# Split row maxima reach Q's rows through a scratch in memory instead of a TensorE transpose

## What is computed

```python
q, k, v = split(x @ W_attn + b_attn)                  # (8, 16, 1024, 32)
scores = einsum('bhki,bhqi->bhkq', k, q) / sqrt(32)   # keys before queries
scores = where(key <= query, scores, -10000.0)
attn = softmax(scores, axis=2)                        # over the keys
x = layernorm(x + combine(attn, v) @ W_out + b_out)
# then a block that routes the top half of the tokens of each of 4 pairs of
# sequences through a 512-2048-512 network, adds, and normalises again
```

## Time and profile before

| | |
|---|---|
| median of 3 runs | 2532.54 us (2531.82 to 2533.45) |
| span of the profiled execution | 2531.8 us |
| PE busy | 2456.4 us, 97% |
| PEld busy | 1817.1 us, 72% |
| DVE busy | 1658.1 us, 65% |
| POOL busy | 1568.4 us, 62% |
| ACT busy | 1191.0 us, 47% |
| DMA packets, data | 167502, 287.45 MB |

### The profile page before, as it was taken

The page is one execution under the profiler, slowest core; times in us unless marked ns, Lnnn a source line. Parts: engine busy times, 40 slices in busy tenths (PEclk is TensorE's granted clock), DMA queues, the critical chain, the costliest instruction groups (busy, mean ns, idle before and its releaser), DMA issues. The chain is left out here.

```text
span 2531.8 us, 40908 instructions
## 1 busy us (share of the span) xinstructions
PE 2456.4 (97%) x14168; PEld 1817.1 (72%) x14168; DVE 1658.1 (65%) x4230; ACT 1191.0 (47%) x2035; POOL 1568.4 (62%) x1642
## 2 busy tenths in 40 slices
PE   8999999999999999999999999997999999999997
PEld 6656676767777677777767667774788888888886
DVE  7767677677767777767787776775655544553533
ACT  3665566556566656656656565566521111111110
POOL 2878778788888788878788887875233122221311
PEclk9999999999999999999999999998999999999999
DMA  4233445335344433535434343443421001010000
GB/s 175 89 127 120 146 141 195 123 127 182 125 147 158 153 134 136 172 131 177 146 124 159 123 172 128 158 146 102 162 80 35 24 26 43 25 34 26 26 25 17
DMA packets 167502, 287.45 MB, mean 114 GB/s; under 512 B 23241, under 2 KB 58121, under 8 KB 166026
## 3 DMA queue, kind: packets, MB, share of 16 engines
q1 hardware_dynamic: 160130, 267.99, 30.2%
q0 software_dynamic: 7168, 16.85, 2.1%
HBM read 116.97 MB, written 65.11 MB: 72 GB/s over the span
## 5 line engine op out<-in xcount | busy, mean ns | idle before, releaser
L867 POOL TENSOR_TENSOR Pa<-Pa,Pm 128x512 f32<-128x512 f32 (+1 forms) x602 | 744.8, 1262 | 105.8 <-ACT Pm L982 92.4
L1492 PE MATMUL PS<-Qp,Kp 128*128 128x512 f32 (+3 forms) x1536 | 488.8, 354 | 23.4 <-ACT Pm L982 13.1
L1458 PE MATMUL PS<-Kp,Qp 128*128 128x512 f32 (+3 forms) x1536 | 487.4, 352 | 9.1 <-DVE nm L1082 6.4
L982 ACT ACTIVATE Pm<-PS 128x512 f32<-128x512 f32 (+1 forms) x643 | 358.3, 569 | 264.7 <-PE PS L1492 219.4
L1082 DVE TENSOR_REDUCE nm<-PS 128x1 f32<-128x512 f32 x512 | 344.8, 688 | 188.0 <-PE PS L1458 187.7
L867 POOL TENSOR_TENSOR Pa<-Pa,P 128x512 f32<-128x512 f32 (+1 forms) x297 | 368.5, 1265 | 51.0 <-ACT P L982 44.4
L1458 PEld LDWEIGHTS PS<-Kp,Qp 128*128 128x128 f32 x1536 | 278.0, 190 | 110.0 <-issue 34.8
L1492 PEld LDWEIGHTS PS<-Qp,Kp 128*128 128x128 f32 x1536 | 278.0, 190 | 102.9 <-ACT Pa L982 28.9
L1090 DVE CUSTOM_DVE_ANT_0 PS<-PS,maskA 128x384 f32<-128x384 f32 (+3 forms) x512 | 246.4, 509 | 151.4 <-PE PS L1458 150.3
L944 ACT ACTIVATE G<-PS,b1c 128x512 f32<-128x512 f32 x128 | 88.2, 689 | 539.6 <-PE PS L1545 539.6
L1090 DVE CUSTOM_DVE_ANT_0 PS<-PS,maskA,nm 128x384 f32<-128x384 f32 (+3 forms) x512 | 265.1, 554 | 87.6 <-PE PS L1458 83.3
(11 more groups left out here) (149 smaller groups left out, 4229.2 us busy)
## 6 DMA issues: line engine op xcount, KB each, us to landing
Qp<-nat SPq DMA_DIRECT2D x192, 256.0 KB, 2.5
Kp<-nat SPq DMA_DIRECT2D x192, 256.0 KB, 2.9
o_s<-Of SPq DMA_DIRECT2D x64, 256.0 KB, 2.2
Ot<-o_s SPq DMA_DIRECT2D x64, 256.0 KB, 3.0
xb<-in_x SPq DMA_DIRECT2D x64, 256.0 KB, 3.0
h_s<-hs SPq DMA_DIRECT2D x64, 256.0 KB, 2.4
out<-xb SPq DMA_DIRECT2D x64, 256.0 KB, 2.4
x_raw<-in_xt SPq DMA_DIRECT2D x15, 1024.0 KB, 6.3
```

The lines of the kernel that those rows point to most:

```text
L867: e.tensor_tensor(to, to, probs(u, k)[:, h0:h0 + many, 0:w], ALU.add).then_inc(s["padd"], many)
L982: e.activation(probs(u, k)[:, hh[0]:hh[-1] + 1, 0:w], tile_bank(j)[:, 0:len(hh) * w].rearrange("p (h n) -> p h n", n=w), ACT.Exp).then_inc ...
L1458: ins = e.matmul(to, Qp[:, u % 4, h_, qt * P:qt * P + P], Kp[:, (2 * i + k0 // 512) % 4, h_, 0:w], start=True, stop=True)
L1492: ins = e.matmul(tile_bank(j)[:, x_ * w:x_ * w + w], Kp[:, (2 * i + k // 4) % 4, h_, k % 4 * P:k % 4 * P + P], Qp[:, u % 4, h_, 512 - w:51 ...
```

## The change

The entry F leaves the ring. Right behind the last maximum of a unit, DVE splits the 16 columns of `nm` where they are into high and low parts, 128 x 16 each, in a tile `shs` of 128 partitions. SP then issues, one beat after, a DMA that writes the 128 x 32 numbers to a scratch in memory laid out [32, 128], so that tokens lie side by side: each piece of it is four bytes. Three beats after that store is issued (in SP's order), SP waits for it to land and issues one DMA that loads 8 KB into each of the two rows of `Qp`. There are two slots of scratch and of `shs`, one for each parity of the unit. Stream B waits for this one load.

```diff
-F_AT = (15.99, 31.99)
-            ring.append((u // 2 * 2 * BEATS + F_AT[u % 2], ("F", u)))
+            if x[0] == "A" and x[2] == len(chunks(x[1])) - 1:
+                self.shifts[int(p)] = x[1]
-        shs = sb("shs", [16, 2, P], F32R)
+        shs = sb("shs", [P, 2, 2 * HG * 4], F32R)
 # sync
-                for a, x_ in T.ring_in(n - 1):
-                    if x_[0] == "F":
-                        u = x_[1]
-                        e.wait_ge(s["a_max"], a + 1)
-                        for j in range(2):
-                            e.dma_start(Qp[32 * j:32 * j + 1, u % 4, :, :].rearrange("a h (t n) -> a (h t) n", n=P)
-                                        .bitcast(F32), shs[:, j, :].bitcast(F32)).then_inc(s["shift"], 16)
+                if n - 1 in T.shifts:
+                    u = T.shifts[n - 1]
+                    e.wait_ge(s["no_max"], u + 1)
+                    if u >= 2:
+                        e.wait_ge(s["shift"], 16 * (u - 1))
+                    with nc.allow_non_contiguous_dma(reason="the scratch has tokens side by side"):
+                        e.dma_start(mD[u % 2].rearrange("c p -> p c"), shs[:, u % 2, :].bitcast(F32)
+                                    ).then_inc(s["shift_st", u % 2], 16)
+                if n - 4 in T.shifts:
+                    u = T.shifts[n - 4]
+                    e.wait_ge(s["shift_st", u % 2], 16 * (u // 2 + 1))
+                    e.dma_start(Qp[0:64:32, u % 4, :, :].rearrange("a h n -> a (h n)").bitcast(F32),
+                                mD[u % 2].rearrange("(a c) p -> a (c p)", a=2)).then_inc(s["shift"], 16)
 # vector
-                if i == 0 and u >= 2:
-                    e.wait_ge(s["a_mm"], T.ring_no["F", u - 2] + 1)
-            def shift_out(j, u):
-                src = PS[0:16, A_BANKS[j % 3], 0:P]
-                e.wait_ge(s["a_mm"], j + 1)
-                if u:
-                    e.wait_ge(s["shift"], 32 * u)
-                link(e.tensor_copy(shs[:, 0, :], src))
+            def shift_out(u):
+                src = nm[:, u % 2, u % 2, :, :].rearrange("p h t -> p (h t)")
+                e.wait_ge(s["a_max"], T.ring_no["A", u, len(chunks(u)) - 1] + 1)
+                if u >= 2:
+                    e.wait_ge(s["shift_st", u % 2], 16 * (u // 2))
+                link(e.tensor_copy(shs[:, u % 2, 0:16], src))
                 linked()
-                e.tensor_tensor(shs[:, 1, :], src, shs[:, 0, :].bitcast(F32), ALU.subtract).then_inc(s["a_max"], 1)
+                e.tensor_tensor(shs[:, u % 2, 16:32], src, shs[:, u % 2, 0:16].bitcast(F32), ALU.subtract).then_inc(s["no_max"], 1)
 # tensor
-            def transpose_maxima(j, u):
-                e.wait_ge(s["a_max"], T.ring_no["A", u, len(chunks(u)) - 1] + 1)
-                e.wait_ge(s["a_max"], j - 2)
-                e.transpose(PS[0:16, A_BANKS[j % 3], 0:P], nm[:, u % 2, u % 2, :, :].rearrange("p h t -> p (h t)"),
-                            cs["identf"][:]).then_inc(s["a_mm"], 1)
-                    e.wait_ge(s["shift"], 32 * (u + 1))
+                    e.wait_ge(s["shift"], 16 * (u + 1))
 # scratch
+        "m": nc.dram_tensor("m_s", [2, 32, P], F32).ap(),
```

More of the change, by code:

```diff
@@ L279, in streams @@
                 ring.append((self.scored[b] + 0.9, ("S", b)))
-        self.ring, self.ring_no = {}, {}
+        self.ring, self.ring_no, self.shifts = {}, {}, {}
         for j, (p, x) in enumerate(sorted(ring, key=lambda y: y[0])):
@@ L472, in layer @@
         bA, sc, sg = cs["battn"], cs["sc"], cs["sg"]
-        hD, scD, wD, oD = dr["h"], dr["sc"], dr["wqkv"], dr["o"]
+        hD, scD, wD, oD, mD = dr["h"], dr["sc"], dr["wqkv"], dr["o"], dr["m"]
         xr = x.rearrange("b (t p) d -> b t p d", p=P)
@@ L1111, in ring_entry @@
             def ring_entry(j, x_):
-                if x_[0] == "F":
-                    shift_out(j, x_[1])
-                elif x_[0] == "S":
+                if x_[0] == "S":
                     scores_out(j, x_[1])
@@ L1117, in ring_entry @@
                     max_piece(j, *x_[1:])
+                    if x_[2] == len(chunks(x_[1])) - 1:
+                        shift_out(x_[1])
             def evacuate(job):
@@ L1473, in ring_entry @@
             def ring_entry(j, x_):
-                if x_[0] == "F":
-                    transpose_maxima(j, x_[1])
-                elif x_[0] == "S":
+                if x_[0] == "S":
                     transpose_scores(j, x_[1])
@@ L1622 @@
               "wo_hi", "wo_lo", "x_hi", "x_lo", "ones", "rows", "d_mm", "ev_v", "ev_a", "kq_hi", "a_mm", "a_max",
-              "shift", "b_mm", "b_exp", "keep", "padd", "pv", "o_cp", "nln", "rinv", "ot", "os_hi", "os",
+              "no_max", "shift", "b_mm", "b_exp", "keep", "padd", "pv", "o_cp", "nln", "rinv", "ot", "os_hi", "os",
               "lmva", "rs", "hset", "oset", "score", "sge", "sig", "scd", "srow", "srow7", "rank_list", "v_link", "v_rank", "p_link",
@@ L1626 @@
               "ghi", "glo", "dn", "q_clear", "k_ones")
-SLOTTED = {"xraw": 2, "of_st": 2, "nat": 2, "ost": 2, "hst": 2, "xb": 2, "lst": 2, "x0": 4, "rw": 8, "li": 2, "hg": 2, "fo": 4, "no_shift": 4}
+SLOTTED = {"shift_st": 2, "xraw": 2, "of_st": 2, "nat": 2, "ost": 2, "hst": 2, "xb": 2, "lst": 2, "x0": 4, "rw": 8, "li": 2, "hg": 2, "fo": 4, "no_shift": 4}
 def program(nc, x, xt, wqkv, wo, bat, b_out, w_router, W1, b1, W2, b2, out):
```

## The result

| | before | after |
|---|---|---|
| median | 2532.76 us | 2972.33 us |
| span of the profiled execution | 2531.8 us | 2964.8 us |
| PE busy | 2456.4 us | 2529.2 us |
| PE idle (span less busy) | 75.4 us | 435.6 us |
| mean granted clock | 0.990 | 0.924 |

The changed kernel is slower: the ratio of the medians is 1.1733, 95% interval 1.1715 to 1.1752. I had forecast 2519.7 us with 2512 to 2620 as the range. The time lies far outside it.

What follows compares the result with a forecast made beforehand. PE, busy 97% of the span, was taken to bound the kernel. Span 2531.8 less 12.8 for the transposes gave 2519.0, plus 0.7 between span and median about 2519.7 us; all else counted nothing; range 2512 to 2620.

Steps and rivals of the forecast that it cites:

- the price of the store: Store to scratch: 4096 pieces, 256 per DMA engine at 16.2 ns plus 1.4 us, landing after 5.5 us.
- twice the price: Rival, odd units' chain: four-byte writes cost about twice eight-byte reads, landing 7.2 to 9.7 us; middle 2575 us; chance 0.20.
- The upper bound: Store to scratch: 512-byte pieces at 27.8 ns each give a landing after 8.5 us at most.
- The mechanism behind a late store: Odd units: PE, in order, stands at `b_tile`'s wait for all the lateness, 0.5 to 3.0 us a unit; nothing returns it.
- far worse of the same kind: Rival: writes to one spot go strictly one after another; at 40 ns a piece near 2676 us; chance 0.17.
- The other terms of the chain: Odd units, besides the store: DVE 0.45, SP's issue 0.05, wake-up 0.1, load 2.3, PE going on 0.1 us.
- the limit itself: Odd units: the latest store landing that still fits before stream B, 6.7 us or 20.7 ns a piece.
- The gain: PE's 64 transposes go, at 0.20 us each: 12.8 us, bounds 0 to 17.3 us.
- handed back: Rival: PE reaches waits for ACT and POOL 0.2 us sooner and stands there; 2529 to 2532 us; chance 0.06.
- SP's queue: SP's wait for the store delays `Ot`, with 7.4 us to spare; cost nothing unless the store takes 13 us.
- issued in other beats: Why a rival was doubted: large x or weight loads before the store make some odd units late; 2540 us; chance 0.02.
- no rate above keeps them: Even units: over 20 us of room before stream B, so none of the piece rates considered makes them late.

Runs made afterwards that it cites:

- e11: Kernel storing 128-byte rows, plus one DMA reading the scratch in 4096 four-byte pieces into 128 partitions of an unused tile; 2533.56 us, single run.
- e4: Kernel storing 128-byte rows, plus a store of 4096 four-byte pieces, 64 bytes each, to a second scratch, which the load awaits; 2684.63 us.
- e10: Kernel storing 128-byte rows, with odd units storing them ten times, each waiting for the one before to land; 2870.68 us.
- e12: Changed kernel with the same 16 KB stored as 2048 pieces of 8 bytes, maxima landing at other tokens; 2587.1 us in a single run.
- e1: Changed kernel with the same 16 KB stored as 128 rows of 128 bytes, maxima landing at other tokens; 2529.05 us, ratio 0.9982.
- e8: Changed kernel with DVE transposing 32 x 32 blocks and four stores of 32 pieces of 128 bytes, maxima at the right tokens; 2530.38 us.
- e5: Changed kernel with the four-byte store only in even units; odd units store 128-byte rows; 2608.16 us, ratio 1.0300.
- e9: e5 with the even units' store and load four beats later in SP's order, behind the next sequence's load of x; 2566.34 us.
- e3: Changed kernel with the same 16 KB stored as 1024 pieces of 16 bytes, maxima landing at other tokens; 2528.17 us, ratio 0.9981.
- e2: Changed kernel storing and loading only the high part, 2048 four-byte pieces instead of 4096; 2730.49 us, ratio 1.0785.

## Why the prediction was wrong

*The step that failed is the price of the store.* "The store then lands 5.5 us after its issue" was taken from the load of `li`, because 8 bytes is nearest to 4. It landed after 16.3. Two things were wrong with it. The row was of reads, and e11 shows that reads of four bytes keep to it (4.7 us) while writes do not (9.5 us even with 64 bytes each, e4). And it was a row of 512 pieces: the first 2653 of the 4096 writes also started at that rate, and only what came after them, and the 7 us in which nothing started, made the landing. The prediction named the difference ("it writes to memory and not from it") and then gave it no more than a rival at twice the price. The upper bound, 27.8 ns a piece from 512-byte pieces, was again a read.

*The mechanism behind a late store was right.* PE stood at `b_tile`'s wait in all 32 odd units, the wait named the load of `Qp`, and nothing gave it back. The rival "twice the price" named it with its place; "far worse of the same kind" named this case, at 0.17, with 40 ns a piece as its example. It came at 58 ((16.3 - 1.4) / 256). That it goes strictly one after another in one spot is not what the runs show: spread over 256 KB it is still slow.

*The other terms of the chain held.* DVE and the issue took 0.67 us for 0.50. The load with its wake-ups took 3.38 us in the unit shown for 2.5, but its median over the odd units is 2.96 there, and 2.46 in e10 and 2.43 in e12. e12 also gives the limit itself: a store of 7.95 us makes the step 11.05 us in the median, 1.27 over e1's 9.78, so a store of 6.7 us would still have fitted, as the prediction had it.

*The gain was mis-sized.* 12.8 us were forecast for the transposes and e1 has 4.3 us of span: 8.1 us less busy time of PE, and 3.8 us more idle time. The step from one start to the next, 0.20 us, was what the transpose took, not what its absence gives: 0.10, at the places shown, because the matmuls behind it start late in either case, and some of that goes at the next wait for ACT. The rival "handed back" describes the second part; that a transpose is worth 8.1 / 64 = 0.13 us of busy time, and not 0.20, no rival had. I gave it 0.06 and it would have been the likeliest for a store of 128-byte rows; its 2529 to 2532 holds e1, and e8.

*SP's queue was costed at nothing up to a store of 13 us*, on the cover of one load (`Ot`). The loads of x and weights were dismissed as "issued in other beats". The load of x is issued some 4 us behind an even store (e5: 421.89 and 425.90), long before that store has landed; its own median landing is 11.1 us in the changed kernel for 6.3 before. It costs ACT 47 us in the changed kernel, and e5 and e9 show that the stores of even units, where "no rate above keeps them" late, lose 78 and 39 us of span by way of the queue.

*No rival priced the clock.* Each stand of PE of 9 us cost some 2.2 us more of busy time (e10).

The sum as the runs give it, over e1's span, is 437.3 us. 312.4 are PE's waits for the load of `Qp`, which e1 does not have. 2529.2 - 2448.3 = 80.9 are PE's longer busy time for the same matmuls at a mean clock of 0.924 for 0.991. The last 44.0 are PE's other idle time, for what is late behind the stores: its waits for ACT's exponentials in `Pm` are 40.4 us for 16.3, those for DVE's maxima (line 1094) 17.1 for 1.9; the rest is small waits, longer and shorter.

Two readings of the earlier trace rows were careless and bear on nothing: three slices of PE, and not two, are not at nine tenths (the last is at seven), and the weight loads, at 72%, are above the 65% that I gave as the most of any other engine.

The Trainium skill, "DMA: Bandwidth & Descriptors", Specifications, has it that below 512 B a DMA engine does a read-modify-write. The trace bears out that small writes to memory are dear, and shows the rule too coarse to price one: 128-byte rows took 1.4 us and 16-byte pieces 3.4 (e1, e3), both far below 512 B. Whether the slow drain sits in the DMA engines or in memory, no run here shows.

## What to carry to other kernels

Price a DMA by a row of the same direction, the same destination and the same number of pieces; a short burst says how fast pieces are taken in, not when the last one lands. What a removed instruction is worth on the engine that sets the pace is the step from its forerunner to its follower with it and without it, less what the next wait takes back. Before an engine is let wait in front of a queue, list every transfer that the queue holds in the next beats, the rare ones at the edges too.

## What the runs showed of the hardware

Four-byte writes to memory: 4096 of them land after 16.3 us side by side, 10.8 with 16 bytes each, 9.5 with 64 bytes each; the same bytes in 16-byte pieces after 3.4 and in 128-byte rows after 1.4. 4096 four-byte reads into 128 partitions land after 4.7 us (a single run), two loads of 2048 into one partition each after 22.6. In the two stores of four-byte pieces looked at one by one (the changed kernel's at 740.08, e2's at 420.44) the last piece starts more than 7 us before the load behind them can go out. While PE stands for 10 us the granted clock falls from 1.00 to 0.50, and 32 stands of 9 us come with 70.6 us of longer busy time (e10). A 32 x 32 block transpose of a 128 x 32 tile of four-byte values takes DVE 0.21 us.
